# Sixteen-head attentions: a third buffer of exponentials, and the value products of two steps in a row on TensorE

## The chip, the cores and the metric

The kernel runs on one NeuronCore of a Trainium2 chip. The metric is the device time of one execution in microseconds (us). Five engines matter: PE (TensorE, with its weight loads shown as PEld), DVE (VectorE), ACT (ScalarE), POOL (GpSimd) and SP (SyncE, which issues the DMAs here). Each has its own queue and runs it in order; they meet by semaphores.

## The reference

A decoder of four layers works on x of shape 2 x 1024 x 256; each layer is an attention, a cross attention to a context of 154 rows, and a feed-forward part, so there are twelve stages, numbered 0 to 11. Six of them hold a sixteen-head attention with 16 channels a head. The core of each is, as in stage 8:

```python
scores = jnp.einsum('bqhd,bkhd->bhqk', q, k) * scale
probs = jax.nn.softmax(scores, axis=-1)
out = jnp.einsum('bhqk,bkhd->bqhd', probs, v).reshape(B, S, H)
```

Stages 0 and 9 are causal over 1024 keys, stages 8 and 11 are not causal over 1024 keys, and stages 4 and 10 have the 154 context rows as keys (stage 10 with a mask).

## The kernel before

Stages 0, 4, 8, 9, 10 and 11 use the class `Attention` (L454) or a subclass. Its work is cut as follows. A **segment** is one batch with eight of the sixteen heads (four segments). A **unit** is four heads (`g`) with 512 queries (`qb`): sixteen units. A **step** is one unit with one tile of 128 keys: 8 steps a unit over 1024 keys, 2 over 154 keys (the second tile has 26 rows), 4 or 8 in the causal stages. `self.steps` lists them: 128 steps in stages 8 and 11, 96 in stages 0 and 9, 32 in stages 4 and 10.

A step n is, in this order on PE (`pe`, L735 and following): `pe_scores(n, 0)`, two matmuls of 98 or 96 rows by 512 queries in bf16 for two heads, into PSUM banks 0 and 1; then the pieces of `slots[2n]`; `pe_scores(n, 1)`, the same for the other two heads, banks 2 and 3; `pe_values(n - 1)`, the product of the exponentials of the step before with the values, into bank 4; then the pieces of `slots[2n + 1]`. The value product is float32, four matmuls that each use 32 columns of the array, `tile_position=(0, 32 * j)`; the trace shows each as two instructions, eight in all. ACT takes the exponential of each pair of banks into `P[n % 2]` (`act`): it waits for `("score", n, jj)` and, before it overwrites a buffer, for `("pv", n - 2)`. `pe_scores(n, jj)` waits for `("exp", n - 1, jj)`, since there is one PSUM place for each half of a step; `pe_values(n - 1)` waits for `("exp", n - 1, 1)`. When a unit is done, ACT copies bank 4 out (`act_sums`), behind the second exponential of the next unit's first step.

The **pieces** are the rest of the attention, spread over half steps by `place()`. They are: `max` (one matmul of scores per 128 queries, head and half of the keys, whose maximum DVE takes; 32 a unit over 1024 keys, 8 over 154 keys, done for the next unit), `fin1` and `fin2` (the maxima are negated on DVE, turned on PE, and put beside the queries by two copies on ACT and two on DVE), `split` and `turn` (projections of the next segment, 8 splits and 16 turns, within the first three units of a segment; of the turns every second one is copied out by ACT, the others by DVE), and `out` (the result of the unit before is turned and divided by its sum). All pieces that need PSUM take banks 5, 6 and 7 by turns (`bank`, `wait_bank`): a piece waits until the piece three before it has been read. The last segment of a stage has no `split` and no `turn`, and the last unit has no maxima either.

Of the kernel before, what the change touches and what calls it, by code (L numbers as in the profile page):

```python
# [441 lines left out]
class Meet(Stage):  # L442
# [8 lines left out]
    act = dve = pool = sp = pe  # L451


class Attention(Stage):  # L454
# [13 lines left out]
    has_post = False  # L468
    lead = 0.3

    def __init__(self, K, tag, KV, causal):
        self.K, self.tag, self.KV, self.causal = K, tag, KV, causal
        scr = K.scr
        self.qS = [scr.take([8, S], BF16) for _ in range(2)]
        kn = S if KV == S else 160
        self.kS = [scr.take([8, kn], BF16) for _ in range(2)]
        self.nk = (KV + 127) // 128
        self.vE = [scr.take([self.nk, 152]) for _ in range(2)]
        self.vh = [v[:, :, 0:136].rearrange("p t (h e) -> p t h e", e=17) for v in self.vE]
# [240 lines left out]
    def pe_values(self, e, n):  # L720
        K, tag = self.K, self.tag
        u, t = self.steps[n]
        s, g, qb = self.units[u]
        vE = self.vE[s % 2]
        lo = self.first_query(u, t)
        if t == 0 and u > 0:
            e.wait_ge(K.av, (tag, "Oc", u - 1))
        e.wait_ge(K.av, (tag, "exp", n, 1))
        for j in range(4):
            m = e.matmul(K.PS[32 * j:32 * j + 32, 4, lo:512], vE[:, t, 17 * (4 * g + j):17 * (4 * g + j) + 32], self.P[n % 2][:, j, lo:512],  # L730
                         start=t == 0, stop=t == self.tiles(u) - 1, tile_position=(0, 32 * j))
        m.then_inc(K.mm, (tag, "pv", n))

    def pe(self, e):
        e.wait_ge(self.K.gv, (self.tag, "filled"))  # L735
        for p in self.first:
            self.pe_piece(e, p)
        for n in range(len(self.steps)):
            for jj in range(2):
                self.pe_scores(e, n, jj)  # L740
                if jj == 1 and n > 0:
                    self.pe_values(e, n - 1)
                for p in self.slots[2 * n + jj]:
                    self.pe_piece(e, p)
        self.pe_values(e, len(self.steps) - 1)
        self.pe_piece(e, ("out", len(self.units) - 1))


# [69 lines left out]
    def act(self, e):  # L818
        K, tag, PS = self.K, self.tag, self.K.PS
        e.wait_ge(K.gv, (tag, "filled"))  # L820
        for p in self.first:
            self.act_piece(e, p)
        for n, (u, t) in enumerate(self.steps):
            rows = min(128, self.KV - 128 * t)
            lo = self.first_query(u, t)
            if n >= 2:
                e.wait_ge(K.mm, (tag, "pv", n - 2))
            for jj in range(2):
                e.wait_ge(K.mm, (tag, "score", n, jj))
                e.activation(self.P[n % 2][0:rows, 2 * jj:2 * jj + 2, lo:512], PS[0:rows, 2 * jj:2 * jj + 2, lo:512], ACT.Exp,  # L830
                             scale=0.25).then_inc(K.av, (tag, "exp", n, jj))
                if jj == 1 and t == 0 and u > 0:
                    self.act_sums(e, u - 1)
                for p in self.slots[2 * n + jj]:
                    self.act_piece(e, p)
        self.act_sums(e, len(self.units) - 1)
# [555 lines left out]
def stages_4(K):  # L1392
    w = K.W[4]
    row = Row(K, "pk4r", 1024)
    att = Attention(K, "a4", KC, False)
    att.wq = segments_of(w.to[:, 0:1536])
    att.bias = row.to[:, 0:768].rearrange("p (s n) -> p s n", s=2)
    return [row, Fill(att), Norm(K, "n4", K.X, att.O), Wait(w.ready, ("pe",)), Wait(row.ready, ("dve", "pool")), Meet(K, "n4"),
            att, AddBias(K, "bias4", K.X, row.to[:, 768:1024]), Meet(K, "a4"),
            Project(K, "o4", att.O, rows_of(w.to[:, 1536:2048]), K.X)]  # L1400
# [253 lines left out]
class BigCross(Stage):  # L1654
# [20 lines left out]
    rows = [128] * 9 + [26]  # L1675
# [1832 lines left out]
def stages_8(K):  # L3508
    w = K.W[8]
    K.WA.clear()  # L3510
    H = K.WA.take([NT, D])
    l1, l2 = w.to[:, 2048:2050], w.to[:, 2050:2052]
    att = Attention(K, "a8", S, False)
    att.wq = segments_of(w.to[:, 0:1536])
    every_ = ("pe", "act", "dve", "pool")
    out = [Wait(w.ready, every_), Fill(att), Norm(K, "n8", K.X, H), Meet(K, "n8"),
           Rms(K, "n8a", H, att.O, lambda c: l1[:, c:c + 1], 1e-5), Meet(K, "n8a"), att, Meet(K, "a8"),
           Project(K, "o8", att.O, rows_of(w.to[:, 1536:2048]), H), Meet(K, "o8")]
    K.scr.clear()
# [129 lines left out]
def stages_9(K):  # L3649
    w = K.W[9]  # L3650
    K.WA.clear()
    sm = K.WA.take([80])
    BD = K.WA.take([5, 8, 16])
    RQ = K.WA.take([NT, 2, 16])
    att = ShortAttention(K, "a9", S, True)
    att.views(w.to)
    att.sm, att.BD, att.RQ, att.flat = sm, BD, RQ, BD.rearrange("p z h d -> p (z h d)")
    every_ = ("pe", "act", "dve", "pool")
    return [Wait(w.ready, every_), Fill(att), Norm(K, "n9", K.X, att.O), Meet(K, "n9"), Ranks(K, att), Meet(K, "ranks"), att, Meet(K, "a9"),
            ShortOut(K, att)]  # L3660
# [54 lines left out]
def stages_10(K):  # L3715
    w = K.W[10]
    take = K.scr.take
    b1, an = take([NT, KC]), take([NT])
    mq, mT = take([NT, KC], BF16), take([2, 2048], BF16)
    row = take([256])  # L3720
    loads = MaskLoads(K, b1, row)
    att = Attention(K, "a10", KC, False)
    att.wq = segments_of(w.to[:, 0:1536])
    att.mask = (mq, mT, an)
    every_ = ("pe", "act", "dve", "pool")
    return [loads, Fill(att), Norm(K, "n10", K.X, att.O), Wait(w.ready, every_), Wait(loads.ready, every_), Meet(K, "n10"),
            Masks(K, b1, an, mq, mT), Meet(K, "masks"), att, AddBias(K, "bias10", K.X, row), Meet(K, "a10"),
            Project(K, "o10", att.O, rows_of(w.to[:, 1536:2048]), K.X)]
# [238 lines left out]
def stages_11(K):  # L3967
    w = K.W[11]
    K.WA.clear()
    H = K.WA.take([NT, D])  # L3970
    lw = w.to[:, 2048:2056].rearrange("p (z c) -> p z c", z=4)
    zt = K.WA.take([1024])
    row = Row(K, "pk11r", 1024, K.WA)
    att = Attention(K, "a11", S, False)
    att.wq = segments_of(w.to[:, 0:1536])
    att.bias = row.to[:, 0:768].rearrange("p (s n) -> p s n", s=2)
    every_ = ("pe", "act", "dve", "pool")
# [4 lines left out]
    xn = K.view(LOW + 8720, [NT, D])  # L3982
    slots = Slots(K, "s11", 32, 5, Heap(K.view, LOW + 8720 + NT * D, LOW + 8720 + 2 * NT * D), K.xg, K.yg)
    zero = Zero(K, slots, zt)
    norm = Norm(K, "n11b", H, xn, mul=lambda c: lw[:, 2, c:c + 1], add=lambda c: lw[:, 3, c:c + 1])
    moe = Capacity(K, H, norm, slots, yz, ring, zero.zeroed)
    moe_at, K.scr.at = K.scr.at, att_at
    out = [row, zero, Fill(att), Wait(w.ready, every_), Wait(row.ready, every_), Norm(K, "n11", K.X, H), Meet(K, "n11"),
           Norm(K, "n11a", H, att.O, mul=lambda c: lw[:, 0, c:c + 1], add=lambda c: lw[:, 1, c:c + 1]), Meet(K, "n11a"),
           att, AddBias(K, "bias11", H, row.to[:, 768:1024]), Meet(K, "a11"),  # L3990
           Project(K, "o11", att.O, rows_of(w.to[:, 1536:2048]), H), Meet(K, "o11")]
    K.scr.at = moe_at
# [243 lines left out]
```

## Time and profile before

| | us |
|---|---|
| median of 3 runs | 6193.91 |
| lowest, highest | 6181.19, 6195.4 |
| the profiled execution | 6189.34 |
| its span, first to last instruction | 6187.2 |

| engine | busy, us | share of the span |
|---|---|---|
| PE | 5460.8 | 88% |
| PEld | 2995.4 | 48% |
| DVE | 3983.8 | 64% |
| ACT | 2851.2 | 46% |
| POOL | 1759.2 | 28% |

The profile is one execution as the hardware profiler saw it; around its span lie 2.1 us. A share of busy time is a mean over twelve stages with different limits. Matmuls are pipelined and overlap their neighbours, so the length of one is not the spacing from one to the next; the spacing is the difference of two starts. A row of the timeline that says "98*128 98x512" is a matmul of 98 rows on 128 columns of the array with 512 columns streamed; "128*32" is a value product, "96*128" a maximum over 1024 keys, "98*26" the scores of the short key tile.

### The profile page before, as it was taken

The page shows a single profiled execution, that of the slowest core. Times are in us where ns is not written, and L with a number is a line of the kernel's source. Part 1 is how long each engine was busy: PE and PEld are TensorE (multiplying, and loading weights), DVE is VectorE, ACT ScalarE, POOL GpSimd, SP SyncE. Part 2 cuts the span into 40 slices and gives each one's busy share as a digit, 9 for nine tenths or more (in the row PEclk, how much of TensorE's full clock was granted, in tenths as well). Part 3 has the DMA queues.
Part 4 walks back from the last instruction along what each step waited for, and adds up shares of the span by engine and source line. Part 5 has one row for each costly group of instructions (what it writes and reads, how often), then busy time and mean ns, then how long its engine had stood idle before and what let it go on. Part 6 is the DMA issues. An engine that isn't in the chain of part 4 may idle for free.

```text
span 6187.2 us, 76720 instructions
## 1 busy us (share of the span) xinstructions
PE 5460.8 (88%) x30116; PEld 2995.4 (48%) x30132; DVE 3983.8 (64%) x6950; ACT 2851.2 (46%) x4536; POOL 1759.2 (28%) x1903
## 2 busy tenths in 40 slices
PE   7987999999877879998998989997968878799978
PEld 4443454454544546555565653326834444333355
DVE  5666767767466579787986247773257745678632
ACT  4553444444005456656564236672135555366610
POOL 3211333333013117354554012202422122222021
PEclk9998999999788989999999879998979989799989
DMA  1000000000000000000000000003510000000033
GB/s 52 1 3 1 1 1 1 1 1 1 21 11 20 8 28 1 1 1 1 1 1 1 10 1 1 1 1 128 183 40 1 1 17 1 31 1 1 28 100 109
DMA packets 39366, 125.12 MB, mean 20 GB/s; under 512 B 5588, under 2 KB 20940, under 8 KB 32990
## 3 DMA queue, kind: packets, MB, share of 16 engines
q1 hardware_dynamic: 28206, 67.70, 3.1%
q0 software_dynamic: 10800, 52.52, 2.5%
q8 instruction: 238, 3.90, 0.3%
q14 instruction: 122, 1.00, 0.1%
HBM read 99.42 MB, written 24.90 MB: 20 GB/s over the span
## 4 chain that ended last, share of the span: by engine, by line


## 5 line engine op out<-in xcount | busy, mean ns | idle before, releaser
L74 PE MATMUL PS<-SC 128*128 128x128 f32 (+14 forms) x14896 | 2819.5, 428 | 168.4 <-ACT SC L80 59.4
L80 ACT ACTIVATE SC<-PS 128x1024 f32<-128x1024 f32 (+9 forms) x2553 | 1932.5, 782 | 1850.0 <-PE PS L74 1549.9
L74 PEld LDWEIGHTS PS<-SC 128*128 128x128 f32 (+6 forms) x14896 | 1220.5, 130 | 1505.7 <-issue 599.9
L95 DVE TENSOR_REDUCE SC<-PS 128x1 f32<-128x512 f32 (+5 forms) x2368 | 1516.4, 681 | 601.8 <-PE PS L74 589.6
L83 POOL TENSOR_TENSOR SC<-SC 128x1024 f32<-128x1024 f32 (+3 forms) x892 | 1190.0, 1344 | 1489.2 <-ACT SC L80 1243.6
L74 PE MATMUL PS<-AR 128*128 128x128 f32 (+6 forms) x4094 | 1129.1, 389 | 67.4 <-DVE SC L83 15.8
L77 PE MATMUL PS<-AR,SC 128*104 128x128 bf16 (+2 forms) x4660 | 532.6, 259 | 353.5 <-DVE SC L86 182.0
L74 PEld LDWEIGHTS PS<-AR 128*128 128x128 f32 (+2 forms) x4094 | 615.2, 175 | 463.1 <-issue 266.6
L74 PE MATMUL PS<-SC,AR 128*128 128x512 f32 (+6 forms) x1922 | 748.2, 514 | 47.7 <-POOL SC L83 12.8
L77 PEld LDWEIGHTS PS<-AR,SC 128*104 128x104 bf16 (+2 forms) x4660 | 413.2, 137 | 568.4 <-issue 221.5
L98 POOL CAST SC<-SC 128x256 bf16<-128x256 f32 (+2 forms) x696 | 264.1, 407 | 1269.9 <-DVE SC L83 667.1
L92 DVE TENSOR_TENSOR_SCAN SC<-SC,PS 128x512 f32<-128x512 f32 x512 | 610.3, 1234 | 0.0
L80 ACT ACTIVATE SC<-SC 128x512 f32<-128x512 f32 (+7 forms) x870 | 445.1, 563 | 342.8 <-DVE SC L83 154.0
L83 DVE TENSOR_TENSOR SC<-SC 128x1024 f32<-128x1024 f32 (+10 forms) x543 | 410.7, 768 | 107.8 <-ACT SC L80 93.7
L74 PEld LDWEIGHTS PS<-SC,AR 128*128 128x128 f32 (+4 forms) x1938 | 314.2, 174 | 300.0 <-issue 212.2
L74 PE MATMUL PS<-RR 64*128 64x512 f32 (+2 forms) x2688 | 429.7, 441 | 18.9 <-DVE SC L95 18.6
L74 PE MATMUL PS<-AR,SC 128*128 128x256 f32 (+4 forms) x1408 | 381.2, 421 | 13.3 <-DVE SC L86 10.4
L98 DVE COPY SC<-PS 2x512 bf16<-2x512 bf16 (+5 forms) x399 | 208.2, 522 | 216.6 <-PE PS L77 123.4
L83 DVE TENSOR_TENSOR SC<-PS,SC 128x256 f32<-128x256 f32 (+3 forms) x289 | 120.8, 428 | 325.3 <-ACT SC L80 177.2
L74 PEld LDWEIGHTS PS<-AR,SC 128*128 128x128 f32 (+2 forms) x1408 | 256.3, 193 | 130.8 <-issue 79.6
L74 PEld LDWEIGHTS PS<-RR 64*128 64x128 f32 (+1 forms) x2688 | 240.7, 185 | 151.1 <-DVE SC L95 52.0
L101 POOL MEMSET SC<- 128x1664 bf16 (+16 forms) x102 | 66.5, 729 | 807.3 <-DVE AR L83 776.2
(84 smaller groups left out, 2191.7 us busy)
## 6 DMA issues: line engine op xcount, KB each, us to landing
SC<-in_pk11e SPq DMA_DIRECT2D x8, 1152.0 KB
SC<-in_pk11e SPq DMA_DIRECT2D x8, 1028.0 KB, 4.9
xg<-SC SPq DMA_DIRECT2D x16, 512.0 KB, 6.7
SC<-yg SPq DMA_DIRECT2D x16, 512.0 KB, 7.8
yg<-AR SPq DMA_DIRECT2D x8, 512.0 KB, 6.5
AR<-in_pk SPq DMA_DIRECT2D x2, 1562.0 KB, 8.5
AR<-in_pk SPq DMA_DIRECT2D x2, 1538.0 KB, 12.6
AR<-in_pk SPq DMA_DIRECT2D x6, 512.0 KB, 5.0
```

The costliest lines, as they stand in the source:

```text
L74: return Step(self.real and self.real.matmul(*a, **k))
L77: return Step(self.real and self.real.transpose(*a, **k))
L80: return Step(self.real and self.real.activation(*a, **k))
L83: return Step(self.real and self.real.tensor_tensor(*a, **k))
L92: return Step(self.real and self.real.tensor_tensor_scan(*a, **k))
L95: return Step(self.real and self.real.tensor_reduce(*a, **k))
L98: return Step(self.real and self.real.tensor_copy(*a, **k))
L101: return Step(self.real and self.real.memset(*a, **k))
```

## The change

`Attention` gets a third buffer of exponentials, `P[2]`, where a heap for it is named: from the scratch heap in stages 4, 10 and 11, from the weight heap `WA` in stages 8 and 9. Stage 0 keeps two. With three buffers `self.pair` is 2, and `pe` emits the value products only in steps of even n: `pe_values(n - 2)` and `pe_values(n - 1)`, both right behind `pe_scores(n, 1)`. In steps of odd n there is none. ACT's wait before it overwrites a buffer becomes `("pv", n - 3)`. To make room in stage 11, the buffers `A` move to `WA`, and the zeros of the expert scatter (`zt`) and the statistics of two norms to a region that the attention uses later, so ACT and DVE wait for the DMAs of the zeros ahead of that attention.

```diff
     def pe(self, e):
...
         for n in range(len(self.steps)):
             for jj in range(2):
                 self.pe_scores(e, n, jj)
-                if jj == 1 and n > 0:
-                    self.pe_values(e, n - 1)
+                if jj == 1 and n > 0 and n % self.pair == 0:
+                    for m in range(n - self.pair, n):
+                        self.pe_values(e, m)
                 for p in self.slots[2 * n + jj]:
                     self.pe_piece(e, p)
-        self.pe_values(e, len(self.steps) - 1)
+        for m in range(len(self.steps) - self.pair, len(self.steps)):
+            self.pe_values(e, m)
...
-            if n >= 2:
-                e.wait_ge(K.mm, (tag, "pv", n - 2))
+            if n >= len(self.P):
+                e.wait_ge(K.mm, (tag, "pv", n - len(self.P)))
...
+        if third is not None:
+            self.P.append(third.take([4, 512]))
+        self.pair = len(self.P) - 1
...
-    att = Attention(K, "a4", KC, False)
+    att = Attention(K, "a4", KC, False, K.scr)
...
-    zt = K.WA.take([1024])
+
+    spare = Heap(K.view, LOW + NT * D, LOW + 2 * NT * D)
+    zt = spare.take([1024])
...
+    zeroed = Wait(zero.zeroed, ("act", "dve"))
```

What stands in PE's queue, shown in three places. AR and SC are the two halves of the core's memory, PS is PSUM. A count joins neighbours of one shape, so "128x512" rows hold scores and maxima together.

The first place is the last segment of stage 8, about one unit and a half. Before:

```order
L74 MATMUL PS<-SC 32x512 x4
L74 MATMUL PS<-SC 128x512 x8
L74 MATMUL PS<-SC 32x512 x4
L74 MATMUL PS<-SC 128x512 x5
L74 MATMUL PS<-SC 32x512 x4
L74 MATMUL PS<-SC 128x512 x6
L77 MATMUL PS<-AR,SC 128x128 x4
L74 MATMUL PS<-SC 128x512 x2
L74 MATMUL PS<-SC 32x512 x4
L74 MATMUL PS<-SC 128x512 x9
```

The same segment now:

```order
L74 MATMUL PS<-SC 128x512 x11
L74 MATMUL PS<-SC 32x512 x4
L74 MATMUL PS<-AR,SC 32x512 x4
L74 MATMUL PS<-SC 128x512 x17
L74 MATMUL PS<-SC 32x512 x8
L74 MATMUL PS<-SC 128x512 x7
L77 MATMUL PS<-AR,SC 128x128 x4
L74 MATMUL PS<-SC 128x512 x2
L74 MATMUL PS<-AR,SC 32x512 x4
```

A value group (x4) stood behind every 8 or 9 scores and maxima; now two stand in a row behind 17 of them.

The second place is the end of stage 8, the unit without maxima. Before:

```order
L74 MATMUL PS<-SC 128x512 x2
L77 MATMUL PS<-AR,SC 128x128 x4
L74 MATMUL PS<-SC 128x512 x2
L74 MATMUL PS<-SC 32x512 x4
L74 MATMUL PS<-SC 128x512 x4
L74 MATMUL PS<-SC 32x512 x4
```

And now:

```order
L74 MATMUL PS<-SC 128x512 x2
L77 MATMUL PS<-AR,SC 128x128 x4
L74 MATMUL PS<-SC 128x512 x6
L74 MATMUL PS<-SC 32x512 x8
L74 MATMUL PS<-SC 128x512 x8
```

Between two value groups stood the four scores of one step and nothing else; now the eight scores of two steps follow each other with no value product between.

The third place is stage 4, one unit of two steps. Before:

```order
L74 MATMUL PS<-SC 128x154 x8
L74 MATMUL PS<-SC 128x512 x2
L74 MATMUL PS<-SC 32x512 x4
L74 MATMUL PS<-SC 26x512 x2
L77 MATMUL PS<-AR,SC 128x128 x4
L74 MATMUL PS<-SC 128x154 x2
L74 MATMUL PS<-SC 26x512 x2
L74 MATMUL PS<-SC 32x512 x4
L77 MATMUL PS<-AR,SC 128x128 x4
L74 MATMUL PS<-SC 128x154 x6
```

And now:

```order
L74 MATMUL PS<-SC 128x154 x8
L74 MATMUL PS<-SC 128x512 x2
L74 MATMUL PS<-SC 32x512 x8
L74 MATMUL PS<-SC 26x512 x2
L77 MATMUL PS<-AR,SC 128x128 x4
L74 MATMUL PS<-SC 128x154 x2
L74 MATMUL PS<-SC 26x512 x2
L77 MATMUL PS<-AR,SC 128x128 x4
L74 MATMUL PS<-SC 128x154 x6
```

The value group that stood between the second short scores and `fin2` (the second "128x128 x4") has moved up, to stand ahead of the first short scores and `out` (the first "128x128 x4").

## Rows read from the trace of the kernel before

**Rows 1.** Windows, loops of stages 4, 8, 9: length, busy of five engines, clock.

```profile
1908.70:2082.00 173.30, 139.45 (x1104) 73.53 (x1104) 106.71 (x276) 106.21 (x125) 61.77 (x130) 0.93 0.00 1
3707.60:4175.30 467.70, 451.73 (x2616) 150.08 (x2616) 347.08 (x609) 317.96 (x374) 78.73 (x192) 0.99 0.00 1
4617.60:4985.30 367.70, 326.75 (x2568) 147.81 (x2568) 260.51 (x569) 205.69 (x286) 79.20 (x192) 0.98 0.00 1
```

**Rows 2.** Timeline, PE around one value group of stage 8 (start, length, [idle before]).

```profile
3802.52 0.59 PE L74 MATMUL PS<-SC 98*128 98x512 bf16 x2
...
3803.04 0.64 PE L74 MATMUL PS<-SC 128*32 128x512 f32 x4
...
3803.50 0.61 PE L74 MATMUL PS<-SC 128*32 128x512 f32 x4
...
3804.04 0.39 PE L74 MATMUL PS<-SC 96*128 96x512 bf16 x1
```

**Rows 3.** Timeline, PE, stage 4: second half of a group, then 26-row scores.

```profile
1943.02 0.80 PE L74 MATMUL PS<-SC 128*32 128x512 f32 x4
...
1943.44 0.38 PE L74 MATMUL PS<-SC 98*26 98x512 bf16 x1
```

**Rows 4.** Timeline, last segment of stage 8, steps with 5 and with 4 maxima.

```profile
4064.23 0.16 PEld L74 LDWEIGHTS PS<-SC 128*32 128x32 f32 x8 [0.42 <-issue]
4065.22 0.76 PEld L74 LDWEIGHTS PS<-SC 96*128 96x128 bf16 x5 [0.84 <-DVE SC L95]
4065.65 3.08 DVE L95 TENSOR_REDUCE SC<-PS 128x1 f32<-128x512 f32 x5 [0.44 <-PE PS L74]
...
4067.00 0.33 PEld L74 LDWEIGHTS PS<-SC 96*128 96x128 bf16 x3 [0.50 <-DVE SC L95]
...
4067.75 0.16 PEld L74 LDWEIGHTS PS<-SC 128*32 128x32 f32 x8 [0.42 <-issue]
...
4069.89 1.94 ACT L80 ACTIVATE SC<-PS 128x1024 f32<-128x1024 f32 x2 [1.00 <-PE PS L74]
...
4070.68 0.16 PEld L74 LDWEIGHTS PS<-SC 128*32 128x32 f32 x8 [0.42 <-issue]
```

**Rows 5.** Timeline, DVE ahead of the loop of stage 11, one unit of maxima.

```profile
5351.61 19.23 DVE L95 TENSOR_REDUCE SC<-PS 128x1 f32<-128x512 f32 x32 [0.56 <-PE PS L74]
```

**Rows 6.** Timeline, last unit of stage 8, steps without maxima.

```profile
4165.90 0.11 PEld L74 LDWEIGHTS PS<-SC 98*128 98x128 bf16 x2 [0.84 <-ACT SC L80]
...
4166.60 3.90 ACT L80 ACTIVATE SC<-PS 128x1024 f32<-128x1024 f32 x4 [0.33 <-PE PS L74]
4166.87 0.16 PEld L74 LDWEIGHTS PS<-SC 128*32 128x32 f32 x8 [0.42 <-issue]
...
4168.59 0.11 PEld L74 LDWEIGHTS PS<-SC 98*128 98x128 bf16 x2 [0.62 <-ACT SC L80]
...
4171.10 0.16 PEld L74 LDWEIGHTS PS<-SC 128*32 128x32 f32 x8 [0.42 <-issue]
```

**Rows 7.** Windows, two units of stage 8, with and without projections.

```profile
3748.80:3782.50 33.70, 32.42 (x206) 12.65 (x204) 24.76 (x43) 22.28 (x31) 12.39 (x31) 1.00 0.00 0
...
3811.50:3837.20 25.70, 24.87 (x137) 6.92 (x136) 21.94 (x40) 17.71 (x19) 0.00 (x0) 1.00 0.00 1
```

**Rows 8.** Timeline, one unit of stage 4.

```profile
2065.84 1.01 ACT L80 ACTIVATE SC<-PS 26x1024 f32<-26x1024 f32 x1 [0.60 <-PE PS L74]
...
2067.03 1.20 ACT L80 ACTIVATE SC<-PS 2x512 bf16<-2x512 bf16 x2 [0.18 <-PE PS L77]
...
2068.37 1.18 PE L74 MATMUL PS<-SC 96*128 96x154 bf16 x10 [1.12 <-ACT SC L80]
```

**Rows 9.** Windows, a stretch of stage 4.

```profile
2062.00:2064.00 2.00, 2.00 (x10) 0.30 (x2) 0.49 (x3) 1.14 (x2) 0.00 (x0) 0.50 0.00 0
```

**Rows 10.** Timeline: GpSimd behind the fills of stage 4; DMA issues of stage 11.

```profile
1887.24 0.40 POOL L98 CAST SC<-SC 128x256 bf16<-128x256 f32 x1 [14.63 <-PE PS L74]
...
5289.20 8.13 SPq L116 DMA_DIRECT2D yg<-AR  x8
```

More of the change, by code:

```diff
@@ L469, with __init__ @@
     lead = 0.3
-    def __init__(self, K, tag, KV, causal):
+    def __init__(self, K, tag, KV, causal, third=None, parts=None):
         self.K, self.tag, self.KV, self.causal = K, tag, KV, causal
@@ L480, in __init__ @@
         self.P = [scr.take([4, 512]) for _ in range(2)]
+        if third is not None:
+            self.P.append(third.take([4, 512]))
+        self.pair = len(self.P) - 1
         self.O = scr.take([NT, D])
         self.ST = [scr.take([2, 8, 104], BF16) for _ in range(3)]
-        self.A = [scr.take([2, 8, 16]) for _ in range(3)]
+        self.A = [(parts or scr).take([2, 8, 16]) for _ in range(3)]
         self.Oc = scr.take([512])
@@ L729, in pe_values @@
         for j in range(4):
-            m = e.matmul(K.PS[32 * j:32 * j + 32, 4, lo:512], vE[:, t, 17 * (4 * g + j):17 * (4 * g + j) + 32], self.P[n % 2][:, j, lo:512],
+            m = e.matmul(K.PS[32 * j:32 * j + 32, 4, lo:512], vE[:, t, 17 * (4 * g + j):17 * (4 * g + j) + 32], self.P[n % len(self.P)][:, j, lo:512],
                          start=t == 0, stop=t == self.tiles(u) - 1, tile_position=(0, 32 * j))
@@ L825, in act @@
             lo = self.first_query(u, t)
-            if n >= 2:
-                e.wait_ge(K.mm, (tag, "pv", n - 2))
+            if n >= len(self.P):
+                e.wait_ge(K.mm, (tag, "pv", n - len(self.P)))
             for jj in range(2):
                 e.wait_ge(K.mm, (tag, "score", n, jj))
-                e.activation(self.P[n % 2][0:rows, 2 * jj:2 * jj + 2, lo:512], PS[0:rows, 2 * jj:2 * jj + 2, lo:512], ACT.Exp,
+                e.activation(self.P[n % len(self.P)][0:rows, 2 * jj:2 * jj + 2, lo:512], PS[0:rows, 2 * jj:2 * jj + 2, lo:512], ACT.Exp,
                              scale=0.25).then_inc(K.av, (tag, "exp", n, jj))
@@ L3512, in stages_8 @@
     l1, l2 = w.to[:, 2048:2050], w.to[:, 2050:2052]
-    att = Attention(K, "a8", S, False)
+    att = Attention(K, "a8", S, False, K.WA)
     att.wq = segments_of(w.to[:, 0:1536])
@@ L3654, in stages_9 @@
     RQ = K.WA.take([NT, 2, 16])
-    att = ShortAttention(K, "a9", S, True)
+    att = ShortAttention(K, "a9", S, True, K.WA)
     att.views(w.to)
@@ L3721, in stages_10 @@
     loads = MaskLoads(K, b1, row)
-    att = Attention(K, "a10", KC, False)
+    att = Attention(K, "a10", KC, False, K.scr)
     att.wq = segments_of(w.to[:, 0:1536])
@@ L3971, in stages_11 @@
     lw = w.to[:, 2048:2056].rearrange("p (z c) -> p z c", z=4)
-    zt = K.WA.take([1024])
+    spare = Heap(K.view, LOW + NT * D, LOW + 2 * NT * D)
+    zt = spare.take([1024])
     row = Row(K, "pk11r", 1024, K.WA)
-    att = Attention(K, "a11", S, False)
+    att = Attention(K, "a11", S, False, K.scr, K.WA)
     att.wq = segments_of(w.to[:, 0:1536])
@@ L3987, in stages_11 @@
     moe_at, K.scr.at = K.scr.at, att_at
-    out = [row, zero, Fill(att), Wait(w.ready, every_), Wait(row.ready, every_), Norm(K, "n11", K.X, H), Meet(K, "n11"),
-           Norm(K, "n11a", H, att.O, mul=lambda c: lw[:, 0, c:c + 1], add=lambda c: lw[:, 1, c:c + 1]), Meet(K, "n11a"),
+    out = [row, zero, Fill(att), Wait(w.ready, every_), Wait(row.ready, every_), Norm(K, "n11", K.X, H, heap=spare), Meet(K, "n11"),
+           Norm(K, "n11a", H, att.O, mul=lambda c: lw[:, 0, c:c + 1], add=lambda c: lw[:, 1, c:c + 1], heap=spare), Meet(K, "n11a"), zeroed,
            att, AddBias(K, "bias11", H, row.to[:, 768:1024]), Meet(K, "a11"),
```

## The prediction

> **What bounds the kernel now.** I read the windows of the attention loops first. In the loop of stage 8 PE is busy 451.7 of 467.7 us, in that of stage 9 326.8 of 367.7, in that of stage 4 only 139.5 of 173.3 [rows 1]. So the 1024-key stages look bound by PE and the 154-key ones by round trips. But busy PE is not PE at its peak, so I then read starts of single instructions, to see what a step is made of.
>
> Around one value group: the last two scores, each some 0.38 us long, fill 0.59 together, so they begin 0.21 apart, at 3802.52 and 3802.73. From the second to the first value product it is 3803.04 - 3802.73 = 0.31, from there to the second half of the group 0.46, from there to the next maximum 0.54 [rows 2]. In stage 4 the second half of a group (start 1943.02 or a little before) is followed by 26-row scores, whose shape also uses 32 columns, after 0.43 [rows 3]. So a value group costs 0.46 + 0.43 = 0.88 us of its own, plus 0.31 - 0.215 = 0.09 for going in and 0.54 - 0.43 = 0.11 for coming out. **This pair of 0.09 and 0.11, 0.205 us, is what the change can save, once for every two steps.**
>
> Now the step. In the last segment of stage 8 a step with 5 maxima lasts 4067.75 - 4064.23 = 3.52 us and one with 4 lasts 4070.68 - 4067.75 = 2.93 [rows 4]. PE's own work in the latter is 4 scores and 4 maxima of 0.215 (1.72) and a value group of 1.09, 2.81 in all, in the former 3.03. What fills the rest of the former is DVE: PE's loads wait 0.50 us for a TENSOR_REDUCE [rows 4]. The rule for it comes from rows: DVE starts 0.43 after its matmul (4065.22 to 4065.65), it takes maxima 0.60 us apart (19.23 / 32) and needs 0.69 for one [rows 4, 5], PE goes on 0.05 later, and a maximum needs the bank of the one three before. With m maxima between two value groups, the last can start only 0.43 + 0.60 (m - 4) + 0.69 + 0.05 = 1.17 + 0.60 (m - 4) after the first. Add its 0.215, two scores 0.43 and the group 1.09: 2.90 for m = 4 and 3.50 for m = 5, which is the trace within 0.03. **So where maxima are dense, the step is set by three banks and DVE; the value group helps, since DVE empties the banks beside it.**
>
> **The change part by part.**
>
> 1. *Dense maxima, no projections* (6 of the 16 units in stage 8 and in 11). Before, 9 maxima in a pair of steps cost 3.50 + 2.90 = 6.40 (trace 6.45). Now all 9 stand between two double groups: 1.17 + 0.60 x 5 = 4.17, then 0.215 + 0.43, then 0.09 + 2 x 0.88 + 0.11 = 1.97: 6.79 us. **+0.38 a pair** although the switches are fewer: the double group gives DVE 2 us in which it can empty only three banks, and the other group, which it used, is gone. A unit has three such pairs and one in which the maxima pause (+0.2 by the same reckoning): +1.3 a unit, +7.8 a stage.
>
> 2. *The last unit* has no maxima, and PE there waits for ACT. From the first scores of an odd step (4165.90) the first exponential starts 0.70 later, the second 0.92 after that (two take 1.94), ends after 1.02, and PE goes on at 4168.59: 2.69 us [rows 4, 6]. Before, 1.09 of this was filled by a value group; a pair takes 4171.10 - 4166.87 = 4.23. Now it is 2.69, two scores 0.43, double group 1.97: 5.09. +0.86 for each of three pairs, and 0.8 more for the group that now stands ahead of the last step's scores instead of behind: +3.4 a stage.
>
> 3. *Units with projections* (9 of 16): in a unit of 33.7 us DVE is busy 24.8 us (73%), in a dense one 21.9 of 25.7 (85%) [rows 7], and PE has splits and turns to do between the maxima. Here the switch can really be saved: at best 4 x 0.205 = -0.8 a unit, at worst the +1.3 of the dense units. With the pieces in their order and the durations above (each starting at the later of its own engine's last piece and what it waits for; for the old order this gives 33.5 and 25.5 us where the trace has 33.7 and 25.7 [rows 7]) gain and loss nearly cancel: +0.1 a unit in stage 8, +0.4 in stage 11, where DVE adds the bias to each split. +0.9 and +3.6.
>
> Stage 8 then gets 7.8 + 3.4 + 0.9 = +12.1, stage 11 7.8 + 3.4 + 3.6 = +14.8.
>
> 4. *Stage 9*, causal: diagonal tiles have narrower and fewer maxima, so most units change little, between -0.5 and +0.8 laid out in the same way, +3 for 15 units, and +2 in the last, which is bare as in 2. +5.
>
> 5. *Stages 4 and 10.* The value group of an odd step moves from behind the 26-row scores to ahead of them. There it lies on the path: +0.88, and ACT's copy of bank 4, `out` behind it and the scores of the odd step all come 0.88 later. What comes back is little. After the odd step's exponential (2065.84) ACT idles only 0.18 until PE's `fin2`, then copies for 1.20, and PE waits 1.12 for those copies [rows 8]: taking the group away in front lets ACT start at most 0.18 (0.3 by the durations of the layout) sooner and makes PE's wait longer. The switch is not saved either, since 26-row scores use 32 columns and switch by themselves. +0.6 to +0.7 for some 15 units: +9.5 in each, +19. Bounds: 0, if the group hides in its new place, and +0.88 x 15 = +13 each.
>
> 6. *The third buffer by itself*: nothing. `("pv", n - 2)` stood ahead of `pe_scores(n, 0)` in PE's queue, so the wait that is relaxed was over before the scores that ACT also waits for. In stages 4 and 10 GpSimd fills one more buffer; it then idles 14.63 us before it is wanted [rows 10]. In stage 11 ACT and DVE wait for the zeros: the last of eight DMAs is issued by 5297.3 [rows 10], the loop's maxima begin at 5351.6 [rows 5]; 50 us cover it. Cost 0 in both; at worst some 2 us.
>
> The sum is 12.1 + 14.8 + 5 + 19 = **+51 us** on the profiled execution's 6189.34 (span 6187.2): 6240. That execution is 4.6 us below the median of the runs, 6193.91, against which the change will be measured: 6245.
>
> The Trainium skill, in TensorEngine Tiling (Array Packing), Key Properties, says that changing the tiling mode, not just the tile, drains TensorE. The trace agrees: 0.31 and 0.54 us around the group where 0.215 and 0.43 would do [rows 2, 3]. By this rule alone one would forecast the first rival below; it counts the drain and not who waits for whom.
>
> **The rivals.**
>
> *A. PE sets the pace everywhere and the switch is saved in full.* 63 merged pairs in stages 8 and 11 each and 47 in stage 9, 173 x 0.205 = -35 us: 6159. For it: PE's busy share of 97% [rows 1]. Against it: the 0.50 waits for DVE and the 0.62 for ACT inside that busy time [rows 4, 6]. It decides if DVE's banks are emptied faster than 0.60 us apiece or there is slack that I don't see.
>
> *B. Half of it.* Stages 4 and 10 hide the group in its new place (the loop of stage 4 has PE idle for 34 of 173 us), and projections save their 0.8 a unit: 51 - 19 - 2 x 9 x 0.8 - 4.5 = +13: 6207, hardly to be told from no change.
>
> *C. The clock falls in more stretches.* In stage 4 it was at 0.50, the lower of its two levels, from 2062 to 2064, a few us behind one of PE's waits, and 0.93 in the mean [rows 9, 1]. Longer waits of PE there and in the last units could add such stretches; each of 2 to 3 us costs 1 to 1.5. Ten of them: +13 more, 6258. The Trainium skill (TensorE: Matmul & The Clock Gate, A second HAM failure mode) describes small idles between groups of matmuls that make the clock swing. No row of the 1024-key units shows it (their windows have 1.00 [rows 7]), so it would concern stages 4 and 10.
>
> *D. The order doesn't change*, or a stage keeps two buffers: excluded by the queue of the changed kernel, where groups of eight stand in all five stages.
>
> **How the numbers follow.** Forecast (slower by 30 to 65 us) 0.72, C 0.09, B 0.11, A 0.08. A measurement of this kernel can tell some 0.3%, 18.6 us, from no change; slower is above 6212.5, faster below 6175.3. B lies about evenly on the two sides of 6212.5 with its spread. Slower 0.72 + 0.09 + 0.03, same 0.08 + 0.01, faster 0.07. The range reaches from the upper part of B to a full C with all five stages at the top of their bounds: 6208 to 6270.
>
> **What would show it.** In the trace after: two value groups 0.88 us apart with 0.09 ahead and 0.11 behind; in the last segment of stage 8 pairs of 6.8 us and units of 27.0 instead of 25.7; the last unit's pairs at 5.1 instead of 4.23, with PE idle before scores for ACT; units with projections within 0.5 us of before; units of stages 4 and 10 0.6 longer, `out` later and a longer wait of PE behind `fin2`. Stages 0 to 3 and 5 to 7 as before. If the double group took much less than 1.97 us, or units of the last segment stayed at 25.7, step 1 would be wrong; if stage 4 kept its 173 us, step 5.

## The result

| | before | after |
|---|---|---|
| median, us | 6187.97 (4 runs, 6181.19 to 6195.4) | 6260.12 (4 runs, 6252.81 to 6264.05) |
| profiled span, us | 6187.2 | 6259.1 |

The change makes the kernel slower: the ratio is 1.0115, 95% interval 1.0097 to 1.0133. The forecast was 6245 and slower; the time lies within the range, 15 us above the number. The spans differ by 71.9 us where the sum said 51. Of the page of after, the busy times:

```profile
span 6259.1 us, 76604 instructions
...
PE 5489.6 (88%) x30132; PEld 3042.2 (49%) x30132; DVE 3972.8 (63%) x6950; ACT 2853.3 (46%) x4536; POOL 1761.6 (28%) x1905
```

PE's share is 88% as before, and no engine's busy time has moved by over 1.6%: the page of shares does not show where 72 us went. The windows of the attention loops do. Columns as in [rows 1]; stages 4, 8, 9, 10 and 11 after:

```profile
1910.00:2105.30 195.30, 156.44 (x1091) 80.20 (x1095) 106.81 (x275) 105.24 (x124) 61.72 (x130) 0.85 0.00 1
...
3736.50:4208.20 471.70, 443.44 (x2600) 156.57 (x2600) 341.95 (x609) 316.64 (x373) 78.47 (x192) 0.99 0.00 1
4652.40:5024.80 372.40, 323.97 (x2554) 154.67 (x2554) 259.34 (x569) 204.64 (x285) 79.06 (x192) 0.97 0.00 1
...
5100.40:5325.90 225.50, 199.44 (x1455) 114.35 (x1455) 98.93 (x240) 117.34 (x160) 62.12 (x130) 0.90 0.00 1
...
5434.60:5913.30 478.70, 446.61 (x2600) 156.63 (x2600) 354.95 (x657) 305.03 (x325) 87.80 (x196) 0.99 0.00 1
```

And of before, stages 10 and 11, which stand in no group above:

```profile
5059.70:5266.90 207.20, 186.55 (x1456) 100.85 (x1472) 99.89 (x240) 118.04 (x161) 62.21 (x130) 0.99 0.00 1
...
5373.80:5842.30 468.50, 451.44 (x2604) 149.31 (x2608) 361.43 (x657) 304.42 (x325) 87.95 (x196) 0.99 0.00 1
```

The column to look at is the third from the end, the granted clock. In the loops over 1024 keys it is within 0.01 of where it was. In stage 4 it fell from 0.93 [rows 1] to 0.85 and in stage 10 from 0.99 to 0.90.

A window ends where I put it; from here on a loop is measured from the start of its first score to the start of its last, which is up to 2 us shorter. What each loop gained, in us, against the forecast, and in three of the experiments below:

| loop of stage | before | after | forecast | `only_1024` | `only_154` | `third_unpaired` |
|---|---|---|---|---|---|---|
| 0 (not changed) | 352.9 | +2.2 | 0 | +2.0 | +0.2 | +2.0 |
| 4 | 171.3 | +24.0 | +9.5 | +0.2 | +22.7 | -0.3 |
| 8 | 465.4 | +6.1 | +12.1 | +7.0 | -0.3 | -1.0 |
| 9 | 366.6 | +5.6 | +5 | +4.2 | -0.7 | -0.6 |
| 10 | 204.8 | +20.6 | +9.5 | +2.6 | +20.4 | +0.1 |
| 11 | 468.2 | +10.4 | +14.8 | +10.4 | +0.3 | -0.2 |

The loops of after add up to 68.9 of the 71.9 us. Stage 0 reads +2 in several kernels that don't touch it, and the stretch between the loops of stages 4 and 8 differs by -8.5 to +3.7 us from kernel to kernel. Stages 4 and 10 also move by up to 3 us where nothing of theirs was changed: stage 10 of `only_1024` reads +2.6, with 13 us at the lower clock where before had 5. So a few us of a total, and up to 3 of one loop, come and go by themselves; the main readings below are larger, or repeat from unit to unit.

**The dense steps are where the forecast put them.** Weight loads of PE in the last segment of stage 8, after; a group is two halves, so a double group has four. The x8 row stands at the start of the first half, the two x4 rows at the starts of the second and the third; the fourth has no load of its own:

```profile
4119.53 0.16 PEld L74 LDWEIGHTS PS<-SC 128*32 128x32 f32 x8 [0.42 <-issue]
4119.99 0.13 PEld L74 LDWEIGHTS PS<-SC 128*32 128x32 f32 x4 [0.30 <-issue]
4120.42 0.13 PEld L74 LDWEIGHTS PS<-SC 128*32 128x32 f32 x4 [0.30 <-issue]
4121.39 0.76 PEld L74 LDWEIGHTS PS<-SC 96*128 96x128 bf16 x5 [0.84 <-DVE SC L95]
4122.56 0.10 PEld L74 LDWEIGHTS PS<-SC 96*128 96x128 bf16 x1 [0.41 <-DVE SC L95]
4123.16 0.33 PEld L74 LDWEIGHTS PS<-SC 96*128 96x128 bf16 x3 [0.50 <-DVE SC L95]
...
4126.30 0.16 PEld L74 LDWEIGHTS PS<-AR,SC 128*32 128x32 f32 x8 [0.42 <-issue]
...
4131.97 0.16 PEld L74 LDWEIGHTS PS<-SC 128*32 128x32 f32 x8 [0.42 <-issue]
```

From the first value product to the next maximum it is 4121.39 - 4119.53 = 1.86 us, that is 0.46 + 0.43 + 0.43 + 0.54 (the matmuls of the fourth half start at 4120.85 in the trace); the working had 1.88. The pair of steps with 9 maxima takes 4126.30 - 4119.53 = 6.77 us, where the working had 6.79 and before had 6.45 [rows 4]. What fills it is DVE's line of maxima:

```profile
4121.82 5.47 DVE L95 TENSOR_REDUCE SC<-PS 128x1 f32<-128x512 f32 x9 [1.30 <-PE PS L74]
4128.59 0.69 DVE L95 TENSOR_REDUCE SC<-PS 128x1 f32<-128x512 f32 x1 [1.30 <-PE PS L74]
```

DVE takes nine maxima without a pause, 5.47 us, and then idles 1.30 behind the double group: 6.77 together, the whole pair. Before, it idled 0.44 behind each single group, ahead of five maxima [rows 4] and, in the same view, of four:

```profile
4069.18 2.48 DVE L95 TENSOR_REDUCE SC<-PS 128x1 f32<-128x512 f32 x4 [0.44 <-PE PS L74]
```

which is 0.44 + 3.08 + 0.44 + 2.48 = 6.44. Two short pauses of the engine that sets the step have become one long one.

**So is the last unit.** PE's loads and ACT in the last unit of stage 8, after:

```profile
4200.38 0.16 PEld L74 LDWEIGHTS PS<-AR,SC 128*32 128x32 f32 x8 [0.42 <-issue]
...
4202.23 0.55 PEld L74 LDWEIGHTS PS<-SC 98*128 98x128 bf16 x4 [0.84 <-ACT SC L80]
4202.94 1.94 ACT L80 ACTIVATE AR<-PS 128x1024 f32<-128x1024 f32 x2 [1.31 <-PE PS L74]
4204.01 0.11 PEld L74 LDWEIGHTS PS<-SC 98*128 98x128 bf16 x2 [1.24 <-ACT AR L80]
...
4204.93 0.11 PEld L74 LDWEIGHTS PS<-SC 98*128 98x128 bf16 x2 [0.80 <-ACT AR L80]
...
4205.46 0.16 PEld L74 LDWEIGHTS PS<-SC 128*32 128x32 f32 x8 [0.42 <-issue]
```

ACT idles 1.31 us behind each double group, since PE does nothing for it meanwhile, and then PE idles for ACT. A pair takes 4205.46 - 4200.38 = 5.08 us (forecast 5.09, before 4.23 [rows 6]).

**Stage 4 is not.** One of its units after, PE's idle time and its loads:

```profile
2070.40 0.80 PE L74 MATMUL PS<-SC 96*128 96x154 bf16 x5 [1.59 <-ACT SC L80]
...
2073.05 0.20 PEld L74 LDWEIGHTS PS<-SC 128*32 128x32 f32 x8 [0.83 <-issue]
...
2073.91 0.19 PEld L74 LDWEIGHTS PS<-SC 128*32 128x32 f32 x4 [0.66 <-issue]
...
2074.76 0.19 PEld L74 LDWEIGHTS PS<-SC 128*32 128x32 f32 x4 [0.66 <-issue]
```

and windows of 1 us through the same stretch:

```profile
2071.00:2072.00 1.00, 0.74 (x9) 0.48 (x8) 0.91 (x3) 0.84 (x1) 0.00 (x0) 0.90 0.00 0
2072.00:2073.00 1.00, 1.00 (x4) 0.21 (x2) 0.97 (x4) 0.18 (x1) 0.00 (x0) 0.50 0.00 0
2073.00:2074.00 1.00, 1.00 (x9) 0.29 (x12) 0.57 (x3) 0.84 (x1) 0.00 (x0) 0.50 0.00 0
2074.00:2075.00 1.00, 1.00 (x12) 0.29 (x8) 0.00 (x0) 0.18 (x1) 0.00 (x0) 0.50 0.00 0
2075.00:2076.00 1.00, 1.00 (x9) 0.19 (x2) 0.00 (x0) 0.00 (x0) 0.00 (x0) 0.89 0.00 0
2076.00:2077.00 1.00, 0.60 (x8) 0.19 (x3) 0.00 (x0) 0.90 (x2) 0.00 (x0) 1.00 0.00 0
```

PE waits 1.59 us for ACT's copies (1.12 before, [rows 8]), and 1.4 us after it works again the clock falls to 0.50, the lower of its two levels (1.2 GHz, where the upper is 2.4), for some 3.4 us: three whole windows and 0.2 us in each neighbour. The mean of the unit agrees: 10.2 us at 0.83 is (1 - 0.83) x 2 x 10.2 = 3.5. The double value group falls into just that stretch: its halves are 0.86 and 0.85 us apart, not 0.46 and 0.43.

### The profile page after: what moved, and what is told of

Same layout as the page of the kernel before. It is cut to its first block, busy times and chain, and to the rows that moved or that the text cites. A ratio compares the mean times of both kernels' runs of the same rounds, so it can differ in the third digit from the quotient of the medians.

```text
span 6259.1 us, 76604 instructions
## 1 busy us (share of the span) xinstructions
PE 5489.6 (88%) x30132; PEld 3042.2 (49%) x30132; DVE 3972.8 (63%) x6950; ACT 2853.3 (46%) x4536; POOL 1761.6 (28%) x1905
## 4 chain that ended last, share of the span: by engine, by line
## 5 line engine op out<-in xcount | busy, mean ns | idle before, releaser
L74 PE MATMUL PS<-SC 128*32 128x512 f32 (+11 forms) x14304 | 2772.8, 425 | 217.2 <-ACT SC L80 85.7
L80 ACT ACTIVATE SC<-PS 128x1024 f32<-128x1024 f32 (+10 forms) x2405 | 1805.1, 773 | 1870.5 <-PE PS L74 1579.7
L74 PEld LDWEIGHTS PS<-SC 128*128 128x128 f32 (+5 forms) x14304 | 1230.6, 131 | 1518.3 <-issue 643.3
L83 POOL TENSOR_TENSOR SC<-SC 128x1024 f32<-128x1024 f32 (+4 forms) x804 | 1147.8, 1437 | 1498.9 <-ACT SC L80 1254.0
L74 PE MATMUL PS<-AR 128*128 128x128 f32 (+6 forms) x4094 | 1136.1, 391 | 75.2 <-DVE SC L83 18.3
L74 PE MATMUL PS<-SC,AR 128*128 128x512 f32 (+7 forms) x1938 | 768.9, 520 | 44.3 <-POOL SC L83 12.6
L98 POOL CAST SC<-SC 128x256 bf16<-128x256 f32 (+3 forms) x560 | 213.9, 408 | 999.3 <-DVE SC L83 394.1
L83 DVE TENSOR_TENSOR SC<-SC 128x1024 f32<-128x1024 f32 (+11 forms) x535 | 407.8, 774 | 98.8 <-ACT SC L80 84.6
L74 PE MATMUL PS<-AR,SC 128*128 128x256 f32 (+4 forms) x2000 | 452.8, 461 | 13.3 <-DVE SC L86 10.4
L74 PEld LDWEIGHTS PS<-AR,SC 128*128 128x128 f32 (+2 forms) x2000 | 272.1, 169 | 165.0 <-issue 113.7
L101 POOL MEMSET SC<- 128x16 bf16 (+15 forms) x105 | 70.9, 741 | 895.6 <-DVE AR L83 865.6
```

The lines of the kernel that those rows point to most:

```text
L74: return Step(self.real and self.real.matmul(*a, **k))
L80: return Step(self.real and self.real.activation(*a, **k))
L83: return Step(self.real and self.real.tensor_tensor(*a, **k))
L98: return Step(self.real and self.real.tensor_copy(*a, **k))
L101: return Step(self.real and self.real.memset(*a, **k))
```

## The experiments

All carry the shared code of the change or none of it, and were timed beside the kernel before. In short:

| kernel | median, us (runs) | before beside it | ratio (95% interval) |
|---|---|---|---|
| `only_1024` | 6215.78 (4) | 6190.45 | 1.0042 (1.0026 to 1.0059) |
| `only_154` | 6235.56 (4) | 6190.45 | 1.0076 (1.0060 to 1.0093) |
| `third_unpaired` | 6194.43 (10) | 6190.45 | 1.0008 (0.9998 to 1.0018) |
| `middle` | 6142.12 (4) | 6190.45 | 0.9923 (0.9907 to 0.9940) |
| `only_154_fill` | 6216.97 (6) | 6190.84 | 1.0040 (1.0028 to 1.0053) |
| `half_max_single` | 6107.12 (2) | 6190.84 | 0.9863 (0.9838 to 0.9888) |
| `half_max_double` | 6111.27 (2) | 6190.84 | 0.9869 (0.9843 to 0.9896) |
| `before_fill` | 6220.06 (5) | 6192.19 | 1.0045 (1.0031 to 1.0059) |
| `middle_more` | 6138.27 (5) | 6192.19 | 0.9916 (0.9902 to 0.9929) |

### By stage: `only_1024`, `only_154` and `third_unpaired`

`only_1024` leaves stages 4 and 10 as before:

```diff
-    att = Attention(K, "a4", KC, False, K.scr)
+    att = Attention(K, "a4", KC, False)
...
-    att = Attention(K, "a10", KC, False, K.scr)
+    att = Attention(K, "a10", KC, False)
```

> The change in stages 8, 9 and 11 alone; stages 4 and 10 keep two buffers and single value groups. Theory (the 1024-key loops lose to DVE and its three banks, the 154-key loops lose to something of their own): the loops of 8, 9 and 11 grow by 6, 6 and 10 us as in the trace of after, stages 4 and 10 keep 171 and 205 us, the whole is +20 to +27 us over before. Rival (what stages 4 and 10 lost in the trace of after is a disturbance of that execution or comes from stage 8 on): the whole stays near +70.

`only_154` is the other half, with the third buffer in stages 4 and 10 alone.

> The change in stages 4 and 10 alone. Theory: their loops grow by some 20 to 24 us each as in the trace of after, the others keep their times, the whole is +42 to +50 us. My forecast's own size for these two was +19 together: if the whole is below +25, what I saw in after was not made by the change. In units whose window has clock 1.00 the difference should be +0.5 us a unit, the rest in units with a lower clock.

`third_unpaired` has the buffer in all five stages and the old order on PE:

```diff
-        self.pair = len(self.P) - 1
+        self.pair = 1
```

> Three buffers of exponentials in all five stages, with all that was moved in memory for them, and the exponentials wait for the value product three steps back, but single value groups in every step as before. Theory (the buffer and the moves cost nothing, the order alone counts): within 0.1% of before, 0 +- 6 us. Rival (the moves in stage 11, the wait for the zeros or a buffer in the other half of memory cost something): +5 to +20.

The buffer by itself and the moved heaps cost nothing that can be told from zero: the interval, -1 to +11 us, still reaches into the rival's range, but the loops of the five stages take no longer than before, and the stretch between the loops of stages 10 and 11, where the waits for the zeros stand, takes 109.2 us in both. So it is the order. The two halves add up: +25.3 and +45.1 by the medians, 70.4 together, against +72.2 for the whole change. And the loops (table above) reproduce those of after within 2 us, each in its own stages. Two thirds of the loss sit in stages 4 and 10, where the sum had put 19 of 51.

### What sets the dense steps: `half_max_single` and `half_max_double`

Both take each maximum of stages 8 and 11 over the first 256 of its 512 columns only, with a smaller scale in the exponential so that it stays finite; the maxima and the probabilities of these stages are not the reference's. PE's work is the same, DVE's for a maximum is about 0.38 us instead of 0.60. `half_max_single` has the order of before, `half_max_double` that of `only_1024`.

```diff
-                e.tensor_reduce(m2[:, i // 4, i % 4, half:half + 1], o, AX.X, ALU.max)
+                e.tensor_reduce(m2[:, i // 4, i % 4, half:half + 1], o if self.causal else o[:, 0:256], AX.X, ALU.max)
```

> The kernel before, but in stages 8 and 11 DVE takes each maximum over 256 of the 512 columns (and the exponentials have another scale, so that nothing overflows): the maxima are not those of the reference, and a reduction costs some 0.33 us apart instead of 0.60. Theory: dense units fall from 25.7 to about 23.2 us, since PE no longer waits for banks. Baseline for the next kernel.

> The same cheap maxima in stages 8 and 11, with the change in stages 8, 9 and 11. Theory (the double group loses because DVE cannot use it): with cheap maxima the dense units are as long as with single groups, 23.2 us, within 0.3, instead of 0.93 longer; the bare last unit still loses some 3 us. Rival (the double group loses by ACT's turn or by something in the group itself): dense units stay 0.9 us longer than with single groups. If the switch saving were all, they would be 0.8 shorter.

One dense unit of stage 8, first `half_max_single`:

```profile
4052.82:4076.18 23.36, 23.36 (x137) 7.35 (x136) 14.12 (x39) 17.50 (x19) 0.00 (x0) 1.00 0.00 1
```

then `half_max_double`:

```profile
4068.05:4091.12 23.07, 22.76 (x137) 7.77 (x137) 13.95 (x40) 17.25 (x20) 0.00 (x0) 1.00 0.00 1
```

With DVE out of the way the unit falls from 25.67 to 23.36 us, PE is busy all of it, and the same change of order that cost 0.93 us a unit now gains 0.29. This shows that the loss in dense units is DVE's. It also shows that rival A's saving is real but small even then: 0.29 of the 0.82 that four switches should give. By the starts of the value groups three of the unit's four pairs save 0.12, 0.24 and 0.16 us, and the one in which the maxima pause takes 0.23 more: PE's loads wait 0.80 us for ACT there. The last unit, which has no maxima, loses what it lost: 16.81 to 19.75 us. In the sum over stage 8 the two nearly cancel (433.3 and 432.0 us).

### The clock in stages 4 and 10: `only_154_fill` and `before_fill`

If the loss there beyond the forecast is the clock, then work that is good for nothing but keeps PE occupied should make the kernel faster. `only_154_fill` is `only_154` with four more products, of the shape of scores, in each odd step, where the value group used to stand; bank 4, which they write, is overwritten by the next value group.

```diff
+    def pe_fill(self, e, n):
...
+        for k in range(4):
+            e.matmul(self.K.PS[:, 4, :], self.kS[s % 2][0:QM, 4 * g + k, 0:128], self.qS[s % 2][0:QM, 4 * g + k, 512 * qb:512 * qb + 512],
+                     start=True, stop=True)
...
+                if jj == 1 and self.pair == 2 and n % 2 == 1:
+                    self.pe_fill(e, n)
```

> The change in stages 4 and 10 alone, and in each odd step, where the value group has gone, four more matmuls of the scores' shape (0.86 us) into the bank of the value products, which is free there; their result is overwritten. It is work added for nothing. Theory (most of the loss in stages 4 and 10 is a clock that falls because PE waits longer in one place): mean granted clock of the two loops back towards 0.93 and 0.99, and the loops no longer, or shorter, than without the added work: some 10 to 25 us less than the kernel with the change in stages 4 and 10 alone. Rival (the loss is the length of the path, ACT's copies behind the value group): the added work costs 0 to 0.9 us a unit, so 0 to +28 us more.

Loops of stages 4 and 10, first `only_154`:

```profile
1910.20:2104.50 194.30, 155.26 (x1095) 79.37 (x1096) 106.79 (x276) 105.12 (x124) 61.52 (x130) 0.85 0.00 1
5076.80:5302.10 225.30, 195.12 (x1439) 108.74 (x1455) 98.90 (x240) 117.29 (x160) 61.94 (x130) 0.92 0.00 1
```

then `only_154_fill`:

```profile
1915.60:2101.60 186.00, 153.83 (x1156) 80.83 (x1160) 106.57 (x276) 105.84 (x125) 61.74 (x130) 0.93 0.00 1
5079.70:5296.10 216.40, 196.79 (x1504) 108.12 (x1520) 99.75 (x240) 117.62 (x161) 61.96 (x130) 0.99 0.00 1
```

The clock is back at the 0.93 and 0.99 of before, and the loops are 8.3 and 8.9 us shorter with 64 products more in each. In a unit of stage 4 with the extra products PE waits 1.11 us for ACT, and the double group runs at the upper level, its halves 0.46 and 0.43 us apart:

```profile
2078.53 1.18 PE L74 MATMUL PS<-SC 96*128 96x154 bf16 x10 [1.11 <-ACT SC L80]
```

```profile
2080.64 0.16 PEld L74 LDWEIGHTS PS<-SC 128*32 128x32 f32 x8 [0.42 <-issue]
2081.10 0.13 PEld L74 LDWEIGHTS PS<-SC 128*32 128x32 f32 x4 [0.30 <-issue]
2081.53 0.13 PEld L74 LDWEIGHTS PS<-SC 128*32 128x32 f32 x4 [0.30 <-issue]
```

The 1.11 us are the wait of before (1.12), not that of `only_154` (1.58), and in stage 10 it is 0.91 instead of 1.54. So this experiment gives PE more work and shorter waits at once. It shows that the loss beyond the layout goes when the clock comes back, not which of the two brings the clock back.

`before_fill` has the same extra products and nothing of the change:

```diff
+                if jj == 1 and self.KV != S and n % 2 == 1:
+                    self.pe_fill(e, n)
                 if jj == 1 and n > 0:
                     self.pe_values(e, n - 1)
```

> The kernel before, with nothing of the change, but with the same four extra score-shaped products (98 rows by 512 queries, bank 4, overwritten by the value group behind them) in every odd step of stages 4 and 10 that only_154_fill had. They leave the result of the kernel as it is. It prices the extra products alone, so that only_154_fill less before_fill is what the change costs in stages 4 and 10 with the clock at its upper level in both. Theory (the layout costs some 0.6 us a unit and the lower clock the rest): the 16 x 4 products of 0.215 us each cost up to 13.8 us a stage and at least nothing, stage 4 some +5 (0 to 14) and stage 10 some +3 (0 to 14), so only_154_fill's +14.4 and +11.4 leave 8 to 11 us a stage for the layout, and the granted clock of stages 4 and 10 stays at 0.93 or more and 0.99. Time 6199 (6190 to 6216). Rival (the extra products lie in idle time and cost nothing, and the layout alone costs 14 and 11 us a stage, so that the layout of the prediction was wrong by half): both loops within 1 us of before, 6190.

Theory and rival both missed, the theory's range of time (6190 to 6216) too: the loops of `before_fill` are 19.7 and 14.1 us longer than before, more than those of `only_154_fill` (14.4 and 11.4), so the subtraction that I had announced gives less than nothing. The reason is visible unit by unit. One unit of stage 10 without projections:

| | value group | extra products | clock | us |
|---|---|---|---|---|
| before | old place | no | 1.00 | 10.53 |
| `before_fill` | old place | yes | 1.00 | 11.50 |
| `only_154`, after | new place | no | 1.00 | 11.02 |
| `only_154_fill` | new place | yes | 1.00 | 11.26 |
| `only_154` | new place | no | 0.79 | 13.58 |

In the old order the four products (0.86 us by 0.215 each) lie on the path and cost 0.97. In the new order they stand where the value group has left a gap and cost 0.24, since PE only waits less for the same copies of ACT. Their price is not the same in the two orders, and a difference of differences is no measure. But the table has what I was after, without it: at the upper clock in both, the change costs 11.02 - 10.53 = 0.49 us in this unit. Two windows of `only_154`, the fourth and the thirteenth unit of stage 10, which run the same instructions:

```profile
5125.30:5138.88 13.58, 11.82 (x74) 6.02 (x74) 5.77 (x15) 5.84 (x7) 0.00 (x0) 0.79 0.00 0
5261.73:5272.75 11.02, 9.40 (x75) 4.67 (x74) 5.50 (x15) 5.84 (x7) 0.00 (x0) 1.00 0.01 1
```

2.56 us between them with the same busy time of ACT and nearly the same of DVE: what differs is the clock. In stage 4 no unit of `only_154` runs wholly at the upper level; there 8.80 us of `only_154_fill`, less the 0.24, against 7.94 before give +0.6, and the unit takes 9.98 at a clock of 0.83.

### A better place for the value group: `middle` and `middle_more`

If DVE sets the dense steps and has three banks to empty while PE does something else, PE's other work should come in pieces too short for DVE to run dry. Before, the value group stands right behind two scores, so that 0.43 + 1.09 = 1.52 us without a maximum come in one piece, and the change makes that 2.4. `middle` is the kernel before with the group put in the middle of the pieces of the second half step, in all six attentions; no third buffer. Now maxima stand between the two scores and the group.

```diff
-                if jj == 1 and n > 0:
-                    self.pe_values(e, n - 1)
-                for p in self.slots[2 * n + jj]:
+                pieces = self.slots[2 * n + jj]
+                ahead = len(pieces) // 2 if jj == 1 else 0
+                for p in pieces[:ahead]:
+                    self.pe_piece(e, p)
+                if jj == 1 and n > 0:
+                    self.pe_values(e, n - 1)
+                for p in pieces[ahead:]:
                     self.pe_piece(e, p)
```

> Two buffers and single value groups as before, but the value group stands in the middle of the pieces behind the second scores of a step instead of ahead of them, in all six attentions. Theory (what counts in dense units is how evenly DVE gets its maxima beside the value groups): the opposite of the change, PE gets from one bank wait to the next with a group between. The layout by the durations of the prediction gives -19 us in stage 8, -20 in 11, -6 each in 9 and 0, -4 each in 4 and 10: -40 to -60 us in all, dense units of 23.9 us instead of 25.7. Rival (the switches and ACT's turn set the pace, not the banks): same number of switches, so within 0.3% of before, dense units still 25.7.

A dense stretch of stage 8 in `middle`, loads of PE:

```profile
4058.68 0.16 PEld L74 LDWEIGHTS PS<-SC 128*32 128x32 f32 x8 [0.28 <-issue]
4059.68 1.42 PEld L74 LDWEIGHTS PS<-SC 96*128 96x128 bf16 x8 [0.84 <-DVE SC L95]
4061.52 0.16 PEld L74 LDWEIGHTS PS<-SC 128*32 128x32 f32 x8 [0.42 <-issue]
...
4064.67 0.16 PEld L74 LDWEIGHTS PS<-SC 128*32 128x32 f32 x8 [0.23 <-issue]
```

and DVE in it:

```profile
4058.80 3.86 DVE L95 TENSOR_REDUCE SC<-PS 128x1 f32<-128x512 f32 x6
4062.95 5.09 DVE L95 TENSOR_REDUCE SC<-PS 128x1 f32<-128x512 f32 x8 [0.30 <-PE PS L74]
```

Eight loads of maxima and scores follow each other without a wait (1.42 us for the eight), and DVE takes 6 and then 8 maxima with 0.30 of idle time between. The pair takes 4064.67 - 4058.68 = 5.99 us instead of 6.45, a dense unit 24.20 instead of 25.67, stages 8 and 11 17.9 and 18.3 us less, stage 0 7.1 less, and the kernel 48 us: 6142, 0.8% faster than before and 1.9% faster than the change. Stages 4, 9 and 10 take 4.6, 2.0 and 1.3 us less where the layout had 4, 6 and 4, so the gain outside the dense units was in part put too high.

`middle_more` puts the larger half ahead where the number of pieces is odd, `ahead = (len(pieces) + 1) // 2`.

> As middle, but of an odd number of pieces behind the second scores the larger half, not the smaller, stands ahead of the value group. Theory (the value group is cover during which DVE empties three banks, so what counts is that the maxima ahead of it and behind it are even): laid out by the durations of before, stages 8 and 11 each take 1.7 us less than in middle, stage 9 the same, stage 4 takes 1.6 and stage 10 4.6 more, since there the pieces ahead of the group put off the next exponentials: 6145 (6138 to 6152), not to be told from middle's 6142. Rival (the gain of middle grows with every piece that moves ahead): under 6130.

Stages 8 and 11 take 0.9 and 1.0 us less than in `middle`, stage 4 takes 3.1 and stage 10 4.1 more: the signs of the layout by durations. Of stage 10's 4.1 us one unit with 3.4 us at the lower clock makes some 1.6, so that its size is near the layout's 4.6 is in part chance. The median is 3.9 us lower than `middle`'s, which is less than the few us that come and go; the two can't be told apart. The gain does not go on growing with each piece moved ahead.

## Why the prediction was right, and where its terms were off

The direction, the mechanism in the long stages and the range held; the sum was 21 us short, and the terms were off on both sides. The loops over 1024 keys were forecast at +31.9 and gained 22.1, those over 154 keys at +19 and gained 44.6: 10 us too much hid part of 26 too little. The number came as near as 15 us by that and because the median of before in the result is 6 us under the one that the forecast started from. The measured 6260 is nearest to the 6258 of rival C, and that the range took it in owes something to luck.

1. *Price of a double group*: 1.88 forecast, 1.86 in the trace. Right.
2. *Dense maxima*: +0.38 a pair forecast, 6.77 - 6.45 = +0.32 in the trace. The pair in which the maxima pause was put at +0.2; it takes 4131.97 - 4126.30 = 5.67 us where before it took 5.72, so nothing. That makes +0.93 a unit instead of +1.3, and 2 us less in each of stages 8 and 11. `half_max_double` shows the cause as named.
3. *The last unit*: 5.08 a pair against 5.09; 19.74 against 16.81 us, +2.9 instead of +3.4.
4. *Units with projections*: +0.1 and +0.4 forecast for a unit, between -0.5 and +0.6 measured: the three of a segment are -0.5, +0.3 and 0.0 in stage 8 and +0.4, +0.6 and -0.2 in stage 11. The first unit of stage 8 took 2.4 us less; it takes 38.8 to 41.2 in kernels of either order, and I count that as nothing.
5. *Stage 9*: +5 forecast, +5.6 measured; its last unit +1.9 of the +2.
6. *Stages 4 and 10*: +9.5 each forecast, +24.0 and +20.6 measured. **This is the term that was mis-sized.** Its layout was right: +0.6 to +0.7 a unit forecast, +0.49 to +0.6 at the upper clock, 8 to 10 us a stage. What the step took from the profile as given was the clock. Unit by unit, (1 - clock) x 2 x length gives the time at the lower level: 23 us of stage 4's loop before and 59 after, 5 of stage 10's before and 43 after. These 74 us more carry the other 14 and 13 us of the two stages.
7. *The third buffer by itself*: nothing, as `third_unpaired` shows (+4 us, interval -1 to +11).

Rival C had named this, with the row for it [rows 9], and was priced too low: ten stretches of 2 to 3 us and +13 us. There are some 22 more of them, of 3.4 us, for +27. I gave C 0.09 because no row of before showed the lower level as a standing guest of a unit; but the same step of the working said that PE's wait behind `fin2` would grow, and that layout is the same in every unit of its kind, so the wait grows in all of them. Rival A is refuted by the rows of DVE above and holds, at a third of its size, only where DVE is relieved. Rival B is refuted: of the group's 0.88 us in its new place 0.49 to 0.6 stay even at the upper clock, and units with projections save at most 0.5.

The Trainium skill (TensorE: Matmul & The Clock Gate, HAM oscillation — how this bites in real kernels) describes loops in which a wait in each pass lets the clock fall again in each pass. The trace agrees in the pattern: three units of stage 4 after in a row, of 9.9 to 10.2 us, have a clock of 0.83 each. In the page's example the wait is one of 3 to 5 us for a DMA. Here it is one of 1.59 us for ACT, and in stage 10 the clock does not fall in every unit.

## What to carry to other kernels

PE's work that feeds no other engine is cover for the one that sets the pace, but only for as long as that engine has something buffered: put it in pieces shorter than that, with its feed between them. Joining two such pieces saved 0.2 us of switching a pair, and with that saving counted still lost 0.3 us a pair where DVE set the pace and 0.9 where ACT did; moving each away from the other idle piece beside it gained 0.46. Where PE has regular waits and the granted clock is already not 1.00, a change that lengthens the waits should be priced a second time with the clock falling in each pass: here 0.5 us of layout a unit became 1.3 to 1.5 in the mean. Stage 10 shows that a clock of 0.99 before is no safeguard.

## What the runs showed of the hardware

Extra products that nobody reads made a kernel faster (6235.56 to 6216.97 us beside nearly the same before); the granted clock of the two loops was 0.93 and 0.99 with them and 0.85 and 0.92 without. What exactly lets it fall stays open: PE waits 1.54 us ahead of the maxima both in the unit of `only_154` at 0.79 and in that at 1.00, so the length of that wait alone does not decide, and in after the fourth unit of stage 10 ran at 1.00 where it stood at 0.79 in `only_154`. The change makes the wait longer with the same work of PE, and the clock falls; the extra products shorten the wait and add work, and it comes back. No run shortened the wait without adding work.

Between two value groups in a row there is no switch: 0.43 us from half to half. The way out of a double group is the same 0.54 us as out of a single one.
